# A four-stage language-model tower on one Trainium2 core: index-decoding blocks at other heads, feed-forward outputs added bank by bank, own PSUM banks at the entry of block attention, the next normalisation inside its last rounds, and the output stored by tile

## The chip, the cores and the metric

The kernel runs on one core of one Trainium2 chip. Five engines of the core work side by side and meet only at semaphores: TensorE (PE in the profile), VectorE (DVE), ScalarE (ACT), GpSimd (POOL), and SyncE (SP), which issues the DMAs. The metric is the device time of one execution in microseconds (us), the median of several runs.

## The reference, cut to what matters

```python
h = tok_ref(x, Wq, Wk)                       # 4 layers of causal attention over one-hot tokens
h = h + attn_ref(layernorm(h), ...)          # RWKV time mixing, 16 heads of 128, scan over time
h = h + ffn_ref(layernorm(h), w1, b1, w2, b2)    # ternary weights, gelu, 512 -> 2048 -> 512
h = h + moba_ref(layernorm(h), Wq, Wk, Wv, Wo)   # block attention, 16 heads of 128
h = h + glu_ref(layernorm(h), lut, gate_idx, up_idx, down_idx)  # silu(gate) * up, weights lut[idx]
```

There are 2048 tokens (8 sequences of 256) of width 512. In the last stage the three weight matrices (1376 x 512 each) are given as indices into a table of 16 numbers.

## The kernel before, in words

`h` (float32) stays in SBUF as 16 tiles of 128 tokens; four tiles are a chunk `c` of 512 tokens, so each stage runs over chunks 0 to 3. Nearly all products are made from a float16 high part and a float16 low part of each operand: one operand's tile is evicted from PSUM by ScalarE (high part) and then by VectorE (low part, value minus high part), and three matmuls (`PASSES`) take the place of one. PSUM has eight banks of 128 x 512 float32; which bank a tile uses decides what it must wait for. The order on every engine is written out by hand; an engine's queue is in order, so that whatever stands behind a waiting instruction waits too.

**Normalisation** (`ln_*`), per chunk: VectorE takes statistics of the four tiles (`bn_stats`, `bn_aggr`, `rstd`), GpSimd raises to -0.5, VectorE writes the normalised tile (`ln_dve_x`), TensorE transposes it (`ln_pe`, four float32 transposes, line 523), ScalarE and VectorE evict the two halves into `tokT` (`ln_act`, line 531; `ln_dve_lo`, line 538). `e` numbers the 64 tiles of the four normalisations.

**Decoding blocks.** The weights of the last stage are decoded by VectorE in blocks of 256 columns (`dec_block`, lines 802 to 820) that are put between other work: after the heads in `RW_DEC` (time mixing) and in `FF_DEC` (feed-forward). SyncE stores each block (`store_dec`) between its own loads of weights.

**Feed-forward**: 64 steps `t`, step `t` being head `t % 16` of chunk `t // 16`. TensorE does `ff_pe_proj(t)` (8 matmuls), then `ff_pe_out(t - 4)` (8 matmuls into banks 4 to 7, summed over the 16 heads of the chunk). After a chunk's last head VectorE adds the four banks to `h` (`ff_dve_acc`), and TensorE may begin the next chunk's first output into these banks only then. GpSimd makes the ternary weights just ahead (`ternary`).

**Block attention**: 64 rounds, two passes `p` of eight steps `s` of four heads `j`. One round on TensorE: queries of the next head (line 239, 12 matmuls), a tile of values for the next step (`mo_v`, 12), keys (12, with the transposes of the probabilities, line 261, after the first three), attention times values (line 1112), a tile of the previous step's output (`mo_out`, 12), the next scores. VectorE's softmax chain stands between the scores and the transposes. In the last step (`p` = 1, `s` = 7) there is no `mo_v`. At the entry the values of step 0 are made (four tiles, all in bank `VB`) and chunk 3 is normalised before the first round. After the last round come four output tiles (`mo_out_tail`).

**Gated stage** (`gl_*`): 12 units, each a group of weight tiles and a chunk. TensorE projects unit `t + 1`, then makes the outputs of unit `t`. Between them, before the change, the normalisation of one chunk each. VectorE decodes 18 more blocks meanwhile.

Of the kernel before, what the change touches and what calls it, by code (L numbers as in the profile page):

```python
# [14 lines left out]
P = 128  # L15
# [4 lines left out]
CH = 512  # L20
# [48 lines left out]
def build(nc, a):  # L69
    with ExitStack() as ctx:  # L70
# [42 lines left out]
        def encR(half_, tt):  # L113
# [83 lines left out]
        h_ps, g32, g_hi, g_lo, ff_out, ff_acc = (sem(x) for x in (  # L197
            "h_ps", "g32", "g_hi", "g_lo", "ff_out", "ff_acc"))
# [546 lines left out]
        def rw_dve_acc(dve, c):  # L745
            dve.wait_ge(rw_out, HEADS * (c + 1))
            for j in range(TPC):
# [4 lines left out]
                  (0, 1, 3, 4, 5, 6, 7, 12, 13, 14, 15), (0, 3, 6, 9, 12, 15)]  # L752
        FF_DEC = (3, 11, 17, 20, 25, 28, 33, 36, 41)
# [166 lines left out]
        def ff_pe_out(pe, t):  # L920
# [52 lines left out]
        def ff_pe(pe):  # L973
# [14 lines left out]
            for t in range(NF - FF_LAG + 1, NF):  # L988
# [77 lines left out]
        def mo_v(pe, p, s, j):  # L1066
# [27 lines left out]
        TAIL_BANK = [FB, 0, 1, 2]  # L1094
# [34 lines left out]
        def mo_pe(pe, p, s, j, nround, nstep, rcond, scond):  # L1129
            u = mo_u(p, s, j)  # L1130
            with Maybe(pe, rcond):
                mo_q(pe, *nround, 0)
            with Maybe(pe, scond):
                mo_v(pe, *nstep, j)
            if rcond is None:
                mo_q(pe, *nround, 1, lambda: pe_transpose_probs(pe, u))
            else:
                pe_transpose_probs(pe, u)
                with Maybe(pe, rcond):
                    mo_q(pe, *nround, 1)  # L1140
            if s == 0 and j == 0:
# [894 lines left out]
```

## Time and profile before

| | |
|---|---|
| median of 3 runs | 2507.6 us |
| lowest, highest | 2503.48, 2508.18 us |
| the profiled execution, its own time | 2510.17 us |
| span of the profiled execution | 2508.2 us |
| TensorE busy | 2341.0 us, 93% of the span |
| VectorE busy | 1651.7 us, 66% |
| ScalarE busy | 788.6 us, 31% |
| GpSimd busy | 371.9 us, 15% |

The span runs from the first to the last event of the profile. TensorE is busy nearly everywhere, so the rows to look at are those where it is not: a row of the timeline has, in brackets at its end, how long the engine was idle before it and what released it.

### The profile page before, as it was taken

To read this page: it belongs to the slowest core of one execution; us is meant where nothing else is said; L and a number is where in the kernel's file an instruction comes from. 1 tells how busy PE (TensorE), PEld (TensorE's weight loads), DVE (VectorE), ACT (ScalarE), POOL (GpSimd) and SP (SyncE) were. 2 spreads that over 40 slices of the span, in tenths; PEclk is the share of its full clock that TensorE was granted. 3 is DMA by queue.
4 is the path that set the end of the run, shared out by engine and by line. 5 is a ranking of instruction groups with operands and counts; after the bars stand their busy time and mean duration, and the time that the engine had idled before them with its cause. 6 is when DMAs were issued, how large, how long until landed. Compare 5 with 4: busy or idle time off the path is not lost.

```text
span 2508.2 us, 32499 instructions
## 1 busy us (share of the span) xinstructions
PE 2341.0 (93%) x12610; PEld 1208.1 (48%) x12610; DVE 1651.7 (66%) x3165; ACT 788.6 (31%) x1683; POOL 371.9 (15%) x416
## 2 busy tenths in 40 slices
PE   5877699999999998989989999999999997899999
PEld 3665344444444444434445555555555544444444
DVE  6665599998999777785345555555555565678622
ACT  5565513112122122333333333333333332211111
POOL 2362200000000411630040004002200300400000
PEclk9998899999999999999989999999999998999999
DMA  4545533333332441211010001000100100000001
GB/s 159 182 149 173 186 123 110 126 122 110 122 118 84 160 160 34 76 34 40 1 67 1 1 1 68 1 2 18 51 1 1 51 1 38 18 1 1 1 1 68
DMA packets 50751, 166.71 MB, mean 66 GB/s; under 512 B 4000, under 2 KB 16928, under 8 KB 41632
## 3 DMA queue, kind: packets, MB, share of 16 engines
q1 hardware_dynamic: 50592, 164.56, 18.6%
q8 instruction: 103, 1.69, 0.3%
q14 instruction: 56, 0.46, 0.1%
HBM read 137.28 MB, written 27.26 MB: 66 GB/s over the span
## 4 chain that ended last, share of the span: by engine, by line
PE 81%; DVE 11%; ACT 4%; issue 2%; POOL 1%; DMA 1%; SPq 0%; DVEq 0%; ACTq 0%
PE ps L665 19%; PE ps L239 13%; PE ps L1240 7%; PE ps L1078 7%; PE ps L677 6%; PE ps L1091 6%; PE ps L558 4%; PE ps L933 3%; PE ps L916 3%; PE ps L408 2%; PE ps L253 2%; PE ps L261 2%; PE ps L1112 2%; PE ps L251 1%; PE ps L523 1%
## 5 line engine op out<-in xcount | busy, mean ns | idle before, releaser
L665 PE MATMUL ps<-planes 128*128 128x512 f16 x1224 | 270.0, 379 | 1.5 <-DVE work L722 1.5
L665 PE MATMUL ps<-planes,wa 128*128 128x512 f16 x1080 | 237.8, 379 | 0.8 <-DVE wsc L1863 0.8
L239 PE MATMUL ps<-planes,wa 128*128 128x512 f16 x840 | 200.0, 383 | 5.1 <-DVE planes L1486 5.1
L665 PEld LDWEIGHTS ps<-planes 128*128 128x128 f16 x1224 | 119.6, 98 | 143.4 <-DVE work L722 2.4
L239 PE MATMUL ps<-planes 128*128 128x512 f16 x768 | 183.1, 382 | 1.3 <-issue 1.3
L705 ACT ACTIVATE work<-work 128x512 f16<-128x512 f32 x64 | 40.3, 630 | 439.8 <-DVE work L738 439.8
L665 PEld LDWEIGHTS ps<-planes,wa 128*128 128x128 f16 x1080 | 105.5, 98 | 125.8 <-DVE wsc L1863 0.8
L294 ACT ACTIVATE ps<-ps,nmax 128x128 f32<-128x128 f32 x160 | 54.4, 340 | 312.1 <-DVE nmax L288 312.1
L505 POOL TENSOR_TENSOR rstd<-rstd,half 128x4 f32<-128x4 f32 x16 | 17.2, 1072 | 889.7 <-DVE rstd L500 889.7
L802 DVE TENSOR_SCALAR work<-work,lutx,par 128x256 int32<-128x256 int32 x384 | 136.0, 429 | 0.0
L820 DVE COPY_PREDICATED work<-work 128x1024 f32<-128x1024 int16 x144 | 121.2, 842 | 22.0 <-DVE work L820 1.3
L933 PE MATMUL ps<-wa,work 128*128 128x512 f16 x512 | 123.8, 387 | 5.4 <-DVE h L958 5.4
L916 PE MATMUL ps<-planes,wa 128*128 128x512 f16 x512 | 124.0, 387 | 3.7 <-POOL wa L1038 3.7
L239 PEld LDWEIGHTS ps<-planes,wa 128*128 128x128 f16 x840 | 82.8, 99 | 92.3 <-DVE planes L1486 5.5
L1240 PE MATMUL ps<-planes 128*128 128x512 f16 x528 | 119.6, 386 | 2.8 <-DVE planes L538 2.8
L1240 PE MATMUL ps<-planes,wa 128*128 128x512 f16 x528 | 116.6, 379 | 0.0
L239 PEld LDWEIGHTS ps<-planes 128*128 128x128 f16 x768 | 75.7, 99 | 80.2 <-issue 4.3
L318 DVE TENSOR_TENSOR work<-ps,work 128x768 f16<-128x768 f32 x76 | 72.7, 956 | 58.4 <-ACT work L314 58.4
L677 PE MATMUL ps<-planes,work 128*128 128x512 f16 x408 | 95.1, 383 | 7.3 <-DVE work L743 7.3
L1078 PE MATMUL ps<-planes 128*128 128x512 f16 x384 | 91.1, 388 | 8.1 <-DVE planes L1178 5.5
L1184 DVE TENSOR_TENSOR h<-ps,h 128x512 f32<-128x512 f32 x64 | 44.2, 692 | 81.6 <-PE ps L1091 77.9
L886 POOL TENSOR_SCALAR planes<-stg 128x512 f16<-128x512 f32 x44 | 29.8, 705 | 436.4 <-PE ps L1091 431.2
(192 smaller groups left out, 4326.4 us busy)
## 6 DMA issues: line engine op xcount, KB each, us to landing
planes<-rw SPq DMA_DIRECT2D x17, 2048.0 KB, 7.8
wa<-rw SPq DMA_DIRECT2D x15, 2048.0 KB, 7.2
stg<-in_rw_w SPq DMA_DIRECT2D x32, 512.0 KB, 3.9
stg<-in_ff_w SPq DMA_DIRECT2D x16, 1024.0 KB, 5.1
rw<-wa SPq DMA_DIRECT2D x16, 1024.0 KB, 6.9
stg<-in_mo_w SPq DMA_DIRECT2D x16, 1024.0 KB, 4.8
work<-in_glu_idx SPq DMA_DIRECT2D x48, 128.0 KB, 2.1
glu_dec<-work SPq DMA_DIRECT2D x48, 128.0 KB, 1.7
```

The source lines that it names most:

```text
L239: mm = te.matmul(ps[:, bank, :], w(i, kt), x(j, kt), start=(kt == 0 and n == 0), stop=(kt == KT - 1 and n == 2))
L318: ve.tensor_tensor(pT[1].rearrange("p (b k) -> p b k", b=2), pT_view, pT[0].rearrange("p (b k) -> p b k", b=2), ALU.subtract).then_inc(pT_ ...
L558: mm = te.matmul(ps[:, bank, :], x, y, start=(m == 0), stop=(m == len(pairs) - 1))
L665: mm = te.matmul(ps[:, what, :], rw_w(q, what, i, kt, m), mix[what][j][:, kt, at:at + CH], start=(kt == 0 and z == 0), stop=(kt == KT - 1 ...
L677: mm = te.matmul(ps[:, 4 + j, :], oT[t % 4][x][:, j * P:j * P + P], rw_wo(q, y, m), start=(n == 0 and z == 0), stop=(n == HEADS - 1 and z ...
L802: return ve.tensor_scalar(dec_v[:, j, :].bitcast(I32), dec_idx, lutx[:, j:j + 1], lut[:, 2 * j:2 * j + 1], ALU.bitwise_and, ALU.bitwise_xor)
L820: ins = ve.copy_predicated(pairs[:, :, 0, :], mask, pairs[:, :, 1, :])
L916: mm = te.matmul(ps[:, t % 3, :], slot[:, at:at + P], tokT[x][:, kt, c * CH:c * CH + CH], start=(kt == 0 and x == 0), stop=(kt == KT - 1 a ...
L933: mm = te.matmul(ps[:, 4 + j, :], gT[t % FF_BUF][x][:, j * P:j * P + P], slot[:, PW + m * D:PW + m * D + D], start=(k == 0 and x == 0), st ...
L1078: mm = te.matmul(ps[:, VB, :], tokT[x][:, kt, tt * P:tt * P + P], halves(slot, 2)[y][:, kt * CH:kt * CH + CH], start=(kt == 0 and z == 0), ...
L1091: mm = te.matmul(ps[:, FB, :], x, y, start=(z == 0), stop=(z == len(pairs) - 1))
L1240: mm = te.matmul(ps[:, bank, :], glu_halves(g, piece)[i][:, at:at + P], tokT[j][:, kt, c * CH:c * CH + CH], start=(kt == 0 and z == 0), st ...
```

## The change

Six things are altered.

1. The decoding blocks of the last time-mixing chunk stand after heads 0, 3, 6, 8, 11, 13 (before: 0, 3, 6, 9, 12, 15), those of the feed-forward stage after steps 3, 15, 17, 21, 31, 34, 38, 47, 50 (before: 3, 11, 17, 20, 25, 28, 33, 36, 41).
2. In the feed-forward stage VectorE adds each bank as soon as that bank is complete, and TensorE waits bank by bank.
3. At the entry of block attention the four value tiles get banks 3 to 6, the first is made before the last two feed-forward outputs, and the transposes of chunk 3 get banks 7, 4, 5, 6.
4. The normalisation of chunks 0 and 1 for the gated stage is done in the last eight rounds (`s` = 6, 7), one tile a round, its statistics one tile a round from `s` = 5. This is inside `If` blocks that only the last pass enters. Chunk 2 is normalised among the tail outputs, chunk 3 among the projections of unit 1.
5. The tail outputs use banks 7, 6, 2, 3 (before: 7, 0, 1, 2).
6. The last chunk of the result is stored in four DMAs, one a tile.

```diff
-                  (0, 1, 3, 4, 5, 6, 7, 12, 13, 14, 15), (0, 3, 6, 9, 12, 15)]
-        FF_DEC = (3, 11, 17, 20, 25, 28, 33, 36, 41)
+                  (0, 1, 3, 4, 5, 6, 7, 12, 13, 14, 15), (0, 3, 6, 8, 11, 13)]
+        FF_DEC = (3, 15, 17, 21, 31, 34, 38, 47, 50)
...
         def ln_bank(e):
+            if e < 4:
+                return ps[:, 6 + e % 2, :]
+            if e < 44:
+                return ps[:, 3, :]
+            if e < 48:
+                return ps[:, (7, 4, 5, 6)[e - 44], :]
+            return ps[:, 4 if e < 56 else 4 + e % 2, :]
...
         def ff_pe_out(pe, t):
-            elif k == 0:
-                pe.wait_ge(ff_acc, TPC * c)
             pe.wait_ge(g_lo, t + 1)
             for j in range(TPC):
+                if c > 0 and k == 0:
+                    pe.wait_ge(ff_acc, TPC * (c - 1) + j + 1)
...
+                if k == HEADS - 1 and j < TPC - 1:
+                    mm.then_inc(ff_bank, 1)
             mm.then_inc(ff_out, 1)
...
         def ff_dve_acc(dve, c):
-            dve.wait_ge(ff_out, HEADS * (c + 1))
             dve.wait_ge(b2_added, TPC * (c + 1))
             for j in range(TPC):
+                if j < TPC - 1:
+                    dve.wait_ge(ff_bank, (TPC - 1) * c + j + 1)
+                else:
+                    dve.wait_ge(ff_out, HEADS * (c + 1))
...
         def mo_pe(pe, p, s, j, nround, nstep, rcond, scond):
+            def transposes():
+                if s > 6 or (s == 6 and j > 0):
+                    with last_pair(pe, p, MO_PAIRS):
+                        pe.wait_ge(ln_done, 24 + 4 * s + j)
+                pe_transpose_probs(pe, u)
...
+            if s == 0 and j == 0:
+                pe.wait_ge(ln_done, 48)
...
+            if s >= 6:
+                with last_pair(pe, p, MO_PAIRS):
+                    ln_pe(pe, 3, s - 6, j)
             with Maybe(pe, rcond):
                 pe_scores(pe, mo_u(*nround))
...
         def mo_dve(dve, p, s, j, nround, nstep, rcond, scond, chain):
+            if s >= 6:
+                with last_pair(dve, p, MO_PAIRS):
+                    ln_dve_x(dve, 3, s - 6, j)
...
                 mo_dve_acc(dve, p, s, j)
+            if s >= 6:
+                with last_pair(dve, p, MO_PAIRS):
+                    ln_dve_lo(dve, 3, s - 6, j)
             with Maybe(dve, rcond):
                 dve_max(dve, mo_u(*nround))
                 dve_norm(dve, mo_u(*nround))
+            if s >= 5:
+                with last_pair(dve, p, MO_PAIRS):
+                    dve.wait_ge(mw_acc, 8 + 49 + 4 * (s - 5) + j)
+                    chain(ve.bn_stats(stat[:, j, :], h[:, (s - 5) * TPC + j, :]))
+                    if j == TPC - 1:
+                        ln_dve_rstd(dve, 3, s - 5, chain)
...
-            for c in range(NC):
+            for c in range(NC - 1):
                 sp.wait_ge(wo_acc, 2 + O_GL + 4 * (2 * NC + c) + 4)
...
+            for tt in range(NT - TPC, NT):
+                sp.wait_ge(wo_acc, 2 + O_GL + 4 * 2 * NC + tt + 1)
+                sp.dma_start(a["out"][:, tt:tt + 1, :], h[:, tt:tt + 1, :]).then_inc(out_sem, 16)
```

How instructions move on VectorE at the end of time mixing: heads 13 to 15 of the last chunk, of before. Lines 722 to 738 are one head, line 538 the low half of a transposed tile, 743 the low part that TensorE's output product reads, 802 and 820 belong to a decoding block, 951 is the first low part of the feed-forward stage.

```order
L722 TENSOR_TENSOR work<-work,ps 128x2x256
L743 TENSOR_TENSOR work<-work 128x512
L729 SCALAR_TENSOR_TENSOR work<-wdec,work 128x256 x2
L734 SCALAR_TENSOR_TENSOR work<-work,par 128x512
L738 TENSOR_TENSOR work<-work 128x512
L538 TENSOR_TENSOR planes<-ps,planes 128x4x128
L807 CAST work<-work 128x256
...
L802 TENSOR_SCALAR work<-work,lutx,par 128x256 x8
...
L743 TENSOR_TENSOR work<-work 128x512
L951 TENSOR_TENSOR work<-work 128x512 x2
```

The same place after the change (the line numbers are those of the changed kernel: 752 is what 743 was, 747 was 738, 547 was 538, 962 was 951).

```order
L731 TENSOR_TENSOR work<-work,ps 128x2x256
L752 TENSOR_TENSOR work<-work 128x512
L738 SCALAR_TENSOR_TENSOR work<-wdec,work 128x256 x2
L743 SCALAR_TENSOR_TENSOR work<-work,par 128x512
L747 TENSOR_TENSOR work<-work 128x512
L547 TENSOR_TENSOR planes<-ps,planes 128x4x128
L752 TENSOR_TENSOR work<-work 128x512
L962 TENSOR_TENSOR work<-work 128x512 x2
```

The block no longer stands between head 15 and the last low part. Next, VectorE at the entry of block attention, of before: 958 adds the feed-forward outputs, 1178 is the low part of a value tile, 284 to 288 the row maximum, 495 to 514 the normalisation, 301 to 307 the division by the row sum.

```order
L958 TENSOR_TENSOR h<-ps,h 128x512 x4
L1178 TENSOR_TENSOR planes<-ps,planes 128x512
L284 TENSOR_TENSOR ps<-ps,causal 128x256
...
L288 TENSOR_REDUCE nmax<-ps 128x2
L495 BN_STATS stat<-h 128x6 x4
L498 BN_AGGR mv<-stat 128x2 x4
L500 TENSOR_SCALAR rstd<-mv 128x4
...
L307 TENSOR_TENSOR work<-ps,rinv 128x2x256
L1178 TENSOR_TENSOR planes<-ps,planes 128x512 x3
L514 TENSOR_SCALAR work<-h,mv,rstd 128x512 x4
L538 TENSOR_TENSOR planes<-ps,planes 128x4x128 x4
```

And of the changed kernel (1209 is what 1178 was, 972 was 958, 499 to 521 are the normalisation, 547 was 538).

```order
L1209 TENSOR_TENSOR planes<-ps,planes 128x512
L972 TENSOR_TENSOR h<-ps,h 128x512 x4
L499 BN_STATS stat<-h 128x6 x4
L505 BN_AGGR mv<-stat 128x2 x4
L507 TENSOR_SCALAR rstd<-mv 128x4
L1209 TENSOR_TENSOR planes<-ps,planes 128x512 x2
L521 TENSOR_SCALAR work<-h,mv,rstd 128x512 x4
L1209 TENSOR_TENSOR planes<-ps,planes 128x512
L284 TENSOR_TENSOR ps<-ps,causal 128x256
...
L288 TENSOR_REDUCE nmax<-ps 128x2
L547 TENSOR_TENSOR planes<-ps,planes 128x4x128 x4
```

The normalisation now stands ahead of the value tiles 1 to 3 and of the softmax. Last, TensorE after the last round, of before: 1104 are the tail outputs, 523 transposes, 1240 projections, 558 outputs.

```order
L1104 MATMUL ps<-wa,planes 128x512 x48
L523 MATMUL ps<-ident,work 128x128 x16
L1240 MATMUL ps<-planes 128x512 x96
L523 MATMUL ps<-ident,work 128x128 x16
L1240 MATMUL ps<-planes 128x512 x96
L523 MATMUL ps<-ident,work 128x128 x16
L558 MATMUL ps<-planes,work 128x512 x48
```

And of the changed kernel (532 is what 523 was, 1123 was 1104, 1285 was 1240).

```order
L532 MATMUL ps<-ident,work 128x128 x8
L1123 MATMUL ps<-wa,planes 128x512 x12
L532 MATMUL ps<-ident,work 128x128 x4
L1123 MATMUL ps<-wa,planes 128x512 x12
L532 MATMUL ps<-ident,work 128x128 x4
L1123 MATMUL ps<-wa,planes 128x512 x24
L1285 MATMUL ps<-planes 128x512 x120
L532 MATMUL ps<-ident,work 128x128 x4
L1285 MATMUL ps<-planes 128x512 x24
```

Eight transposes now stand ahead of the first tail output, and no transposes stand between the outputs and the projections.

## Rows read from the trace of the kernel before

**Rows 1.** The page's first line, the span and the instruction count.

```profile
span 2508.2 us, 32499 instructions
```

**Rows 2.** Busy time by stretch of the span, columns as in its first line.

```profile
core 0: us, PE busy (x) PEld busy (x) DVE busy (x) ACT busy (x) POOL busy (x), PEclk, DMA share, GB/s
965.00:1240.00 275.00, 252.71 (x1161) 116.32 (x1159) 184.43 (x335) 97.08 (x149) 73.57 (x84) 0.96 0.12 41
1240.00:1280.00 40.00, 23.33 (x88) 10.41 (x89) 17.69 (x32) 7.67 (x17) 26.80 (x32) 0.74 0.22 79
1280.00:2007.00 727.00, 724.14 (x4317) 394.99 (x4315) 404.77 (x721) 267.54 (x720) 77.45 (x91) 1.00 0.05 18
2007.00:2114.00 107.00, 91.43 (x534) 49.65 (x532) 58.28 (x113) 34.96 (x98) 2.02 (x2) 0.95 0.00 1
2114.00:2241.00 127.00, 109.86 (x498) 52.59 (x499) 88.79 (x197) 24.67 (x41) 31.11 (x38) 0.92 0.07 27
2241.00:2509.00 268.00, 259.52 (x1199) 116.77 (x1197) 137.40 (x283) 39.25 (x64) 13.07 (x24) 0.99 0.04 16
```

**Rows 3.** TensorE's timeline, feed-forward stage: start, length, line, operation, [idle before <-releaser].

```profile
983.21 4.22 PE L677 MATMUL ps<-planes,work 128*128 128x512 f16 x12 [7.29 <-DVE work L743]
...
1023.08 3.00 PE L916 MATMUL ps<-planes,wa 128*128 128x512 f16 x8 [3.71 <-POOL wa L1038]
...
1057.14 2.93 PE L933 MATMUL ps<-wa,work 128*128 128x512 f16 x8 [1.97 <-DVE h L958]
...
1095.12 0.83 PE L523 MATMUL ps<-ident,planes 128*128 128x128 f32 x4 [4.80 <-DVE planes L538]
...
1126.07 3.58 PE L933 MATMUL ps<-wa,work 128*128 128x512 f16 x8 [2.31 <-DVE h L958]
...
1186.05 1.90 PE L933 MATMUL ps<-wa,work 128*128 128x512 f16 x8 [1.11 <-DVE h L958]
```

**Rows 4.** VectorE's timeline, feed-forward stage, and one row of GpSimd's.

```profile
1046.84 0.29 DVE L807 CAST work<-work 128x256 int16<-128x256 int32 x1
...
1053.40 1.28 DVE L951 TENSOR_TENSOR work<-work 128x512 f16<-128x512 f32 x2
...
1061.66 6.44 DVE L802 TENSOR_SCALAR work<-work,lutx,par 128x256 int32<-128x256 int32 x8
...
1179.45 0.69 DVE L951 TENSOR_TENSOR work<-work 128x512 f16<-128x512 f32 x1 [2.76 <-ACT work L947]
...
1003.23 1.38 POOL L505 TENSOR_TENSOR rstd<-rstd,half 128x4 f32<-128x4 f32 x1 [25.01 <-DVE rstd L500]
```

**Rows 5.** TensorE's timeline at the entry of block attention.

```profile
1242.35 4.35 PE L1078 MATMUL ps<-planes 128*128 128x512 f16 x12 [2.58 <-DVE h L958]
...
1280.11 2.75 PE L1078 MATMUL ps<-planes 128*128 128x512 f16 x12
```

**Rows 6.** TensorE's timeline in the rounds, and one row of VectorE's.

```profile
1690.56 2.75 PE L239 MATMUL ps<-planes 128*128 128x512 f16 x12 [1.30 <-issue]
...
2078.90 0.87 PE L261 MATMUL ps<-ident,work 128*128 128x128 f32 x6 [1.69 <-DVE work L307]
...
2052.54 0.69 DVE L1178 TENSOR_TENSOR planes<-ps,planes 128x512 f16<-128x512 f32 x1 [0.37 <-ACT planes L1158]
...
2054.05 0.96 DVE L318 TENSOR_TENSOR work<-ps,work 128x768 f16<-128x768 f32 x1 [0.83 <-ACT work L314]
```

**Rows 7.** TensorE's and VectorE's timelines after the last round.

```profile
2114.47 10.52 PE L1104 MATMUL ps<-wa,planes 128*128 128x512 f16 x48 [0.88 <-DVE h L1184]
...
2186.55 1.94 PE L523 MATMUL ps<-ident,work 128*128 128x128 f32 x8 [5.78 <-DVE planes L538]
...
2240.60 20.88 PE L1240 MATMUL ps<-planes 128*128 128x512 f16 x96
...
2117.53 1.92 DVE L514 TENSOR_SCALAR work<-h,mv,rstd 128x512 f32<-128x512 f32 x4
```

**Rows 8.** VectorE's timeline, its last row.

```profile
2502.79 0.69 DVE L563 TENSOR_TENSOR h<-ps,h 128x512 f32<-128x512 f32 x1 [1.25 <-PE ps L558]
```

More of the change, by code:

```diff
@@ L496, in ln_dve_chunk, with ln_dve_rstd @@
             chain(ins)
+            ln_dve_rstd(dve, f, c, chain)
+        def ln_dve_rstd(dve, f, c, chain):
             for j in range(TPC):
@@ L987, in ff_pe @@
             mo_q(pe, 0, 0, 0, 1)
-            for t in range(NF - FF_LAG + 1, NF):
+            ff_pe_out(pe, NF - FF_LAG + 1)
+            pe.wait_ge(ln_done, 44)
+            mo_v(pe, 0, 0, 0, V_FIRST[0])
+            for t in range(NF - FF_LAG + 2, NF):
                 ff_pe_out(pe, t)
@@ L1064, in mo_q, with mo_v @@
                        lambda i, kt: tokT[i][:, kt, c * CH:c * CH + CH], between)
-        def mo_v(pe, p, s, j):
+        V_FIRST = [3, 4, 5, 6]
+        def mo_v(pe, p, s, j, bank=VB):
             g, c = s // 4, s % 4
@@ L1135, in mo_pe @@
             if rcond is None:
-                mo_q(pe, *nround, 1, lambda: pe_transpose_probs(pe, u))
+                mo_q(pe, *nround, 1, transposes)
             else:
-                pe_transpose_probs(pe, u)
+                transposes()
                 with Maybe(pe, rcond):
                     mo_q(pe, *nround, 1)
-            if s == 0 and j == 0:
-                pe.wait_ge(ln_done, 48)
             mo_pv(pe, p, s, j)
@@ L1876, in _ @@
             dve_k(dve, MU)
+            mo_dve_v(dve, 0, 0, 0, V_FIRST[0])
             ff_dve_acc(dve, NC - 1)
-            mo_dve_v(dve, 0, 0, 0)
-            dve_max(dve, MU)
             dve.wait_ge(ff_acc, TPC * NC)
             ln_dve_chunk(dve, 2, NC - 1, chain)
-            dve_norm(dve, MU)
-            for j in range(1, TPC):
-                mo_dve_v(dve, 0, 0, j)
-            ln_chunk(dve, ln_dve_x, 2, NC - 1)
-            ln_chunk(dve, ln_dve_lo, 2, NC - 1)
-            def mo_dve_round(p, s, j, *rest):
-                mo_dve(dve, p, s, j, *rest)
-                if s >= 5 and j == 3:
-                    with last_pair(dve, p, MO_PAIRS):
-                        dve.wait_ge(mw_acc, 8 + 52 + 4 * (s - 5))
-                        ln_dve_chunk(dve, 3, s - 5, chain)
-            mo_rounds(dve, mo_dve_round)
-            ln_chunk(dve, ln_dve_x, 3, 0)
-            for tt in range(TPC):
-                mo_dve_acc(dve, MO_PAIRS, 0, tt, TAIL_BANK[tt])
-            ln_chunk(dve, ln_dve_lo, 3, 0)
+            mo_dve_v(dve, 0, 0, 1, V_FIRST[1])
+            mo_dve_v(dve, 0, 0, 2, V_FIRST[2])
+            ln_chunk(dve, ln_dve_x, 2, NC - 1)
+            mo_dve_v(dve, 0, 0, 3, V_FIRST[3])
+            dve_max(dve, MU)
+            ln_chunk(dve, ln_dve_lo, 2, NC - 1)
+            dve_norm(dve, MU)
+            mo_rounds(dve, lambda *x: mo_dve(dve, *x, chain))
+            ln_chunk(dve, ln_dve_x, 3, 2)
+            ln_dve_lo(dve, 3, 2, 0), ln_dve_lo(dve, 3, 2, 1)
+            mo_dve_acc(dve, MO_PAIRS, 0, 0, TAIL_BANK[0])
+            ln_dve_lo(dve, 3, 2, 2)
+            mo_dve_acc(dve, MO_PAIRS, 0, 1, TAIL_BANK[1])
+            ln_dve_lo(dve, 3, 2, 3)
+            mo_dve_acc(dve, MO_PAIRS, 0, 2, TAIL_BANK[2])
+            mo_dve_acc(dve, MO_PAIRS, 0, 3, TAIL_BANK[3])
             dve.wait_ge(mw_acc, 8 + 64)
             ln_dve_chunk(dve, 3, 3, chain)
-            ln_chunk(dve, ln_dve_x, 3, 1)
+            ln_chunk(dve, ln_dve_x, 3, 3)
             def gdec_step(t, at):
```

86 lines of the change are left out of this document (47 added, 39 removed).

## The prediction

> **What bounds the kernel now.** I read busy time by stretch first: TensorE sets the pace, and what can be won is where it stands still or runs at the lower clock. Of the span of 2508.2 us [rows 1], the rounds of block attention up to 2007 leave it idle 3 us in 727; nothing is to be had there. The feed-forward stretch (965 to 1240) leaves 22 us, the entry of block attention (1240 to 1280) 17 in 40, at a granted clock of 0.74, the last rounds (2007 to 2114) 16 of 107, the stretch after them (to 2241) 17 of 127, and the rest 8 [rows 2]. Then TensorE's timeline, for each idle time and its releaser: nearly always VectorE, which is behind because a decoding block or a normalisation stands ahead of what TensorE needs. A full-speed group of 8 matmuls of 512 columns takes 1.73 us to the next start, one of 12 takes 2.59; these follow from the starts in the rounds, and behind a wait of 2 us or more the rows are longer (4.22, 3.00, 2.93 and 3.58 us where 2.75 and 1.89 are usual) [rows 3]: the lower clock costs some 1.7 us each time.
>
> **Step a, the end of time mixing.** A block ahead of the last low part holds TensorE 7.29 us, and the 12 matmuls behind it take 4.05 to the next start instead of 2.59 [rows 3]. With the last block after head 13, VectorE has 4.9 us of slack to absorb it, and the low part is done in time: 7.3 + 1.5 = 8.8. Is it given back at the next wait, step 12's weights from GpSimd (3.71 us, [rows 3])? GpSimd stood 25.01 us waiting for the statistics that VectorE takes behind step 4 [rows 4]. These come earlier with the rest, so the wait moves along and stays near 4. I take 8.6. Were GpSimd bound by its weights alone, 0 to 3 would be left.
>
> **Step b, blocks in the feed-forward stage, and bank-by-bank sums.** A block with GpSimd at rest takes 6.56 us (1046.84 to 1053.40); beside GpSimd's splits its eight leaf instructions alone take 6.44 [rows 4], as long as the whole. TensorE can wait for a sum at three places, the first output of chunks 1 to 3. Bank by bank, the first bank is free 0.62 us after VectorE starts instead of 2.48: 1.9 better wherever VectorE is late. But where VectorE is late is set by the blocks. Chunk 1: blocks at 15 and 17 lie so close that the second starts some 1.5 us late and meets GpSimd's split; the sum starts 1056.5 to 1057.5 against 1054.6, the first bank is free at 1058.2, against 1057.14 [rows 3]: 1.0 lost. Chunk 2: the block at 34 is followed by one low part and the sum: TensorE would wait 2.95 instead of 2.31: 0.65 lost. Chunk 3 had no block near; TensorE waited 1.11 [rows 3]. Now low part 50 starts at 1179.45 [rows 4], +0.6 the block, to 1186.6, low part 51, first bank at 1187.85, while TensorE is ready at 1184.94: 2.9 instead of 1.1, plus the lower clock 1.6: 3.4 lost. Against these, the wait of 4.80 at the second transpose of chunk 0 with its slow row [rows 3] goes, as no block stands at 25; the first transpose waits some 3 us longer for block 21: 2.2 won. Sum of b: -2.9, bounds -9 (the first-transpose wait long, each chunk slow) and +4 (blocks hidden by the banks).
>
> **Step c, entry of block attention.** Before: TensorE ends the feed-forward outputs at 1239.8, then four value tiles, each waiting for the eviction of the last (one bank), and four transposes likewise (2.58 idle before the first tile, [rows 5]); the first value tile of round 1 starts at 1280.11 [rows 5]. After, worked forward from 1239.8: value tile 0 stands ahead of the last 16 matmuls, so outputs end at 1242.4; scores to 1243.4; tiles 1 to 3 without a wait (the first bank is added by 1241.7, the last by 1243.6) to 1251.2. VectorE: statistics to 1246.7, GpSimd's power 1.1, two low parts, normalised tiles from 1249.9 at 1.1 to 1.3 each, as GpSimd is splitting. Transposes at 1251.2, 1252.1, 1253.2, and the last at 1255.0 behind low part 3. Softmax maximum to 1256.8, four low halves to 1259.5. TensorE does round 1's queries from 1255.6, slow, to 1260.1, and then the value tile. 1280.1 - 1260.1 = 20. Bounds 14 and 22.
>
> **Step d, the last rounds.** TensorE gets eight groups of four float32 transposes; six such in a row take 0.87 us with their tail, 0.71 to the next start [rows 6], so a group takes 0.47 when fast, the last more: 3.9 in all. In the four rounds of step 7 the softmax is exposed: TensorE waits 1.69 us for it [rows 6]. The low half (0.6 us, as 0.69 with its tail in [rows 4]) now stands ahead of the maximum; it ends about 0.25 us after the scores do: 1.0 for four. In step 6 the added 1.1 us (statistics 0.6, normalised tile 0.5) fall in front of the low part of the probabilities, before which VectorE was idle 0.83, and 0.37 two instructions ahead of it [rows 6]: 1.2 of cover, less the 0.25; I count 0.3 for three rounds. The three former groups of statistics (a wait of 1.6 to 1.7 us each, within the 16 us of this stretch, [rows 2]) become a group with GpSimd's power in the middle: the same. d = -5.2, bounds -4 and -12.
>
> **Step e, from the last round to unit 3.** Counted from the end of the last round's output, 2113.6. Before: the projection of unit 3 starts at 2240.6 [rows 7], 127.0 later. After: work of four tail tiles 10.4, three projections 62.2, two outputs 20.7, eight groups of transposes 3.5 = 96.8. New waits: the first transpose needs one low half, statistics, power and a normalised tile, about 5.0 us after the last output, against 0.9 before the tail [rows 7]; 4.3 idle after one group of transposes. Lower clock 2.5 (two slow groups), small waits 1, an allowance. Together 105. So e = 22. The idle 5.78 us [rows 7] and its like one unit later vanish: they were VectorE, which now has 4 normalised tiles of 0.48 us [rows 7] and 4 low halves of 0.6 [rows 4] fewer there. I take 21.5, bounds 15 and 23.
>
> **Step f, the store.** The last sum ends at 2503.5 [rows 8], the span 4.7 later: issue and a transfer of 1 MB. A 256 KB transfer should land in 2.2 to 2.8 after issue: 1.7, bounds 0.5 and 2.5.
>
> **Branches.** The `If` blocks add some 15 compare-and-branch a pass on TensorE, 28 on VectorE. The rounds before hold such branches too, and are idle 3 us in 727 [rows 2]. Only the jump back of the loop shows, 1.30 us [rows 6]. I take 1 for all. The Trainium skill (Advanced Engine Details and Errata, Control Flow Timing) gives about 108 ns for a compare-and-branch and 51 ns for a plain one; if nothing hid them, TensorE's 30 would cost some 5 us by that page, an estimate, and the sum be 4 us smaller. The trace of the rounds speaks for hidden.
>
> **Sum.** 8.6 - 2.9 + 20 - 5.2 + 21.5 + 1.7 - 1 = 42.7. The profiled execution took 2510.2 by its own time, which gives 2467.5; the median of the runs shown is 2.6 lower, 2507.6, and lies within their spread, so 2465.
>
> **The rivals.** *The likeliest*: gains of 30 to 50 us, 2457 to 2478: 0.76.
> *VectorE becomes late where it has just been loaded.* In rounds of step 7 TensorE would idle 1.94 us, close to the 1.97 after which its rows were slow [rows 3, 6]: 1.7 more each for three rounds; with b at its bound and c at 14: gain 42.7 - 5 - 6 - 6 - 3 = 23, some 2485. For it: VectorE's cover in step 6 is 0.1 us wide. Against: most idle times that are removed are waits by construction. 0.13 (2478 to 2500).
> *The change frees more than I count*: no slow rows at the entry, blocks hidden: 2450 to 2457: 0.07.
> *Slower: the added branches are not hidden.* If each of TensorE's 30 cost what the jump back costs, 1.30 us [rows 6], that is 39 us; with VectorE's in the softmax chain it is above 43 and the kernel comes out at 2508 to 2520. It decides from 1.45 us a branch. Against it: the branches already in the rounds. 0.02. A smaller cost of that kind leaves no change, 0.01; below all that, 0.01.
> *A part doesn't do what it says*: the bank-by-bank sums are covered by the blocks ahead of them, worth nothing at chunks 2 and 3; this is in b.
>
> **How the numbers follow.** Prediction 2465, range 2452 to 2484: the likeliest case, the better one in part, and half of the late one. A difference of 0.2%, 5 us, is about what a measurement here can tell from none. Faster 0.96, within 0.02, slower 0.02.
>
> **What the profile after would show.** a: no idle time in front of line 677's successor at 975. b: waits for `h` at three chunk starts, the third near 2.9 us. c: value tiles back to back, round 1's value tile 20 us nearer to the last feed-forward output. d: rounds of step 6 near 13.6 us, those of step 7 near 13.2. e: one idle time of 4 us ahead of the tail, then none above 1 until unit 3; 105 us from the last round's output to unit 3. f: 3 us from the last sum to the end. It is wrong if GpSimd's weights at step 12 come no earlier, if step-7 rounds run slow, or if the tail waits for more than the statistics.

## The result, and the profile after

| | before | after |
|---|---|---|
| median (4 runs each, in one comparison) | 2507.89 us | 2475.82 us |
| lowest, highest | 2503.48, 2510.07 | 2473.06, 2478.94 |
| ratio, 95% interval | | 0.9873, 0.9857 to 0.9889 |
| profiled execution, own time / span | 2510.17 / 2508.2 | 2473.06 / 2471.1 |

The change gains 32.1 us by the medians, 37.1 by the two profiled spans; forecast were 42.7, a time of 2465 in a range of 2452 to 2484. The profiled execution of after was the fastest of its kernel, that of before slower than all four of its row: 3.2 of the 37.1 us are there before the change has moved anything on TensorE (the time-mixing output at 966.68 before stands at 963.45 after).

Busy time by stretch first (with [rows 2], columns as there): the feed-forward stage, and the entry of block attention, which now lies between 1233 and 1252.

```profile
965.00:1233.00 268.00, 250.50 (x1149) 115.16 (x1148) 169.82 (x318) 97.90 (x150) 75.57 (x84) 0.96 0.12 41
1233.00:1252.00 19.00, 15.87 (x87) 8.14 (x84) 16.04 (x29) 6.91 (x16) 12.16 (x15) 1.00 0.12 44
```

At the entry the granted clock was 0.74 with 17 us idle in 40; now it is 1.00 with 3 idle in 19. The feed-forward stretch still has 17.5 idle. What TensorE waits for, from the view of waits (us in total, times, longest):

```profile
PE ps L942 <- DVE h L972: 9.0, 3, 3.1
PE ps L567 <- DVE h L572: 8.1, 6, 5.3
PE ps L532 <- DVE planes L521: 6.6, 5, 4.5
...
PE ps L925 <- POOL wa L1055: 4.0, 1, 4.0
PE ps L1285 <- DVE work L1323: 2.6, 2, 2.1
```

Lines 567 and 1285 are the gated stage's outputs and projections, and the forecast had no wait of 5.30 or 2.13 us there. TensorE's timeline in the feed-forward stage (with [rows 3]):

```profile
975.11 5.34 PE L925 MATMUL ps<-planes,wa 128*128 128x512 f16 x24
...
1011.21 3.27 PE L925 MATMUL ps<-planes,wa 128*128 128x512 f16 x8 [3.98 <-POOL wa L1055]
...
1045.79 2.31 PE L942 MATMUL ps<-wa,work 128*128 128x512 f16 x8 [2.82 <-DVE h L972]
...
1066.41 1.12 PE L532 MATMUL ps<-ident,planes 128*128 128x128 f32 x4 [4.49 <-DVE planes L521]
...
1113.95 3.57 PE L942 MATMUL ps<-wa,work 128*128 128x512 f16 x8 [3.11 <-DVE h L972]
...
1177.09 3.04 PE L942 MATMUL ps<-wa,work 128*128 128x512 f16 x8 [3.10 <-DVE h L972]
...
1222.06 5.34 PE L239 MATMUL ps<-planes 128*128 128x512 f16 x24
```

The 7.29 us of [rows 3] are gone (step a), and every chunk's first output waits for its sum longer than before (step b). The rows behind two of these waits are slow: 3.57 us at a granted clock of 0.50 and 3.04 at 0.63. The one of chunk 1, 2.31 us, is not: its granted clock is 1.00. It has to wait for VectorE bank by bank, three more banks at 0.62 us each and 0.45 for its last two matmuls, and it takes the same 2.31 us in experiments 1 and 5 behind waits of 0.49, 0.61 and 1.29. The entry (with [rows 5]):

```profile
1235.99 7.93 PE L1097 MATMUL ps<-planes 128*128 128x512 f16 x36
...
1244.74 0.63 PE L532 MATMUL ps<-ident,work 128*128 128x128 f32 x4 [0.37 <-DVE work L521]
...
1247.84 0.66 PE L532 MATMUL ps<-ident,work 128*128 128x128 f32 x4 [1.18 <-DVE planes L1209]
...
1252.16 2.75 PE L1097 MATMUL ps<-planes 128*128 128x512 f16 x12 [1.07 <-DVE planes L547]
```

Three value tiles stand in one row, no wait reaches 1.2 us and no row is slow. The last rounds, step 7 (with [rows 6]):

```profile
2054.40 0.94 PE L261 MATMUL ps<-ident,work 128*128 128x128 f32 x6 [1.93 <-DVE work L307]
2055.14 3.77 PE L239 MATMUL ps<-planes,wa 128*128 128x512 f16 x9
```

The wait for the softmax is 1.93 where it was 1.69, and behind one of three such waits nine matmuls took 3.77 us for 2.10, at a granted clock of 0.55. From the last round on, TensorE, then VectorE and GpSimd beside it (with [rows 7]):

```profile
2095.93 1.92 PE L532 MATMUL ps<-ident,work 128*128 128x128 f32 x8 [4.30 <-DVE work L521]
...
2109.77 26.06 PE L1285 MATMUL ps<-planes 128*128 128x512 f16 x120
...
2144.01 5.35 PE L1285 MATMUL ps<-planes 128*128 128x512 f16 x24 [2.13 <-DVE work L1323]
...
2155.87 5.34 PE L567 MATMUL ps<-planes,work 128*128 128x512 f16 x24
2166.51 7.62 PE L567 MATMUL ps<-planes,work 128*128 128x512 f16 x24 [5.30 <-DVE h L572]
...
2205.79 20.88 PE L1285 MATMUL ps<-planes 128*128 128x512 f16 x96
```

```profile
2091.23 0.69 DVE L1215 TENSOR_TENSOR h<-ps,h 128x512 f32<-128x512 f32 x1 [1.98 <-PE ps L1110]
...
2133.54 1.14 DVE L857 TENSOR_SCALAR planes<-planes 128x256 int16<-128x256 int16 x1
...
2143.28 0.68 DVE L1323 TENSOR_TENSOR work<-work,ps 128x512 f32<-128x512 f32 x1
...
2146.18 0.23 DVE L857 TENSOR_SCALAR planes<-planes 128x256 int16<-128x256 int16 x1
...
2165.77 0.68 DVE L572 TENSOR_TENSOR h<-ps,h 128x512 f32<-128x512 f32 x1
...
2467.96 0.69 DVE L572 TENSOR_TENSOR h<-ps,h 128x512 f32<-128x512 f32 x1 [1.25 <-PE ps L567]
```

```profile
2133.45 4.55 POOL L899 TENSOR_TENSOR wa<-stg,wa 128x512 f16<-128x512 f32 x4
```

TensorE makes two output tiles of unit 0 from 2155.87 and then waits 5.30 us, since the third goes into the bank of the first, which VectorE adds only at 2165.77. VectorE had no idle time above 0.7 us since 2132.8 and is behind. The first decoding block of this stage is one reason: it fills 2132.81 to 2143.28, 10.5 us, where in the kernel before it took 6.2 (2159.40 to 2165.62). Its small instructions take 1.14 to 1.26 us where the first of these lines takes 0.23 at 2146.18, and four of them fill 4.58 us beside four instructions of GpSimd that fill 4.55. The Trainium skill (SBUF — State Buffer, SBUF: two separate sides) says that VectorE and GpSimd share a pair of ports under a lock that one of them holds for a whole instruction, where VectorE's instruction is in a two-port mode or has two inputs in SBUF. The 4.58 against 4.55 us for four each agree with it; of which kind these four are, no run here shows. In the kernel before, GpSimd's splits ended at 2156.5, ahead of that block:

```profile
2151.46 5.00 POOL L890 TENSOR_TENSOR wa<-stg,wa 128x512 f16<-128x512 f32 x4
```

The 37.1 us by the prediction's steps, each from its marker in the one trace to that in the other:

| step | forecast | measured | markers, before and after |
|---|---|---|---|
| before any change | 0 | 3.2 | 966.68, 963.45 |
| a, end of time mixing | 8.6 | 8.9 | 24 matmuls of line 916 / 925: 987.26, 975.11, less 3.2 |
| b, feed-forward | -2.9 | -5.0 | from there to the first queries: 241.98, 246.95 |
| c, entry | 20 | 20.8 | queries to round 1's value tile: 50.87, 30.10 |
| d, last rounds, branches | -6.2 | -5.6 | to VectorE's sum of the last round: 833.52, 839.07 |
| e, to unit 3 | 21.5 | 12.4 | 126.97, 114.56 |
| f, to the end | 1.7 | 2.3 | 267.6, 265.3 |

### The profile page after: what moved, and what is told of

It reads as the page before. It is cut to its first block, busy times and chain, and to the rows that moved or that the text cites. A ratio compares the mean times of both kernels' runs of the same rounds, so it can differ in the third digit from the quotient of the medians.

```text
span 2471.1 us, 32609 instructions
## 1 busy us (share of the span) xinstructions
PE 2327.8 (94%) x12610; PEld 1203.5 (49%) x12610; DVE 1652.3 (67%) x3165; ACT 788.4 (32%) x1683; POOL 374.4 (15%) x416
## 3 DMA queue, kind: packets, MB, share of 16 engines
q8 instruction: 103, 1.69, 0.3%
## 4 chain that ended last, share of the span: by engine, by line
PE 80%; DVE 11%; ACT 5%; issue 2%; POOL 1%; DMA 1%; SPq 0%; DVEq 0%; ACTq 0%
PE ps L674 19%; PE ps L239 13%; PE ps L1285 7%; PE ps L686 7%; PE ps L1110 6%; PE ps L1097 6%; PE ps L567 3%; PE ps L925 3%; PE ps L942 3%; PE ps L408 2%; PE ps L253 2%; PE ps L1131 2%; PE ps L261 2%; PE ps L251 1%; PE ps L532 1%
## 5 line engine op out<-in xcount | busy, mean ns | idle before, releaser
L674 PE MATMUL ps<-planes 128*128 128x512 f16 x1224 | 270.0, 379 | 1.2 <-DVE work L731 1.2
L239 PE MATMUL ps<-planes 128*128 128x512 f16 x768 | 180.9, 379 | 1.5 <-issue 1.5
L1285 PE MATMUL ps<-planes 128*128 128x512 f16 x528 | 116.9, 379 | 2.6 <-DVE work L1323 2.6
L962 DVE TENSOR_TENSOR work<-work 128x512 f16<-128x512 f32 x64 | 49.4, 783 | 73.9 <-ACT work L958 73.9
L301 DVE RECIPROCAL rinv<-rsum 128x4 f32<-128x4 f32 x80 | 14.2, 177 | 119.4 <-ACT ps L296 119.4
```

The costliest lines, as they stand in the source:

```text
L239: mm = te.matmul(ps[:, bank, :], w(i, kt), x(j, kt), start=(kt == 0 and n == 0), stop=(kt == KT - 1 and n == 2))
L674: mm = te.matmul(ps[:, what, :], rw_w(q, what, i, kt, m), mix[what][j][:, kt, at:at + CH], start=(kt == 0 and z == 0), stop=(kt == KT - 1 ...
L1285: mm = te.matmul(ps[:, bank, :], glu_halves(g, piece)[i][:, at:at + P], tokT[j][:, kt, c * CH:c * CH + CH], start=(kt == 0 and z == 0), st ...
```

## The experiments

The changed kernel is at 0.9873 of before; 0.001 is 2.5 us. Ratios are to the kernel before, run on the same chip, and gains against the changed kernel are differences of two such ratios. As each is known to about 0.0016, a difference is good to some 5 us. Experiments 1, 2, 5 and 10 to 12 are clear of the changed kernel; the intervals of 3, 4, 6 and 8 touch or overlap its own, so there the same stretch in two traces is given as well.

**1. The old feed-forward table.**

```diff
-        FF_DEC = (3, 15, 17, 21, 31, 34, 38, 47, 50)
+        FF_DEC = (3, 11, 17, 20, 25, 28, 33, 36, 41)
```

> The changed kernel (2475.8 us) with the feed-forward blocks back after steps 3, 11, 17, 20, 25, 28, 33, 36, 41; the bank-by-bank sums stay. Theory (the new table made the feed-forward stage slower, the sums by bank made it faster): the waits for h at the starts of chunks 1 to 3, now 2.82, 3.11 and 3.10 us, shrink below 0.5 each as 1.9 comes off the 1.97, 2.31 and 1.11 of the kernel before, their slow rows go, and the wait of 4.8 at the second transpose of chunk 0 comes back in place of 4.49 at the first: about 11 us less, 2465. Rival (the sums by bank bring nothing, the tables alone tell): the three waits are 2.0, 2.3 and 1.1 as in the kernel before, 5 us less, 2471.

2465.49 us, 0.9823 (0.9807 to 0.9840): 12.5 us faster than the changed kernel. TensorE's timeline:

```profile
1047.31 2.31 PE L942 MATMUL ps<-wa,work 128*128 128x512 f16 x8 [0.49 <-DVE h L972]
...
1067.26 1.12 PE L532 MATMUL ps<-ident,planes 128*128 128x128 f32 x4 [3.83 <-DVE planes L521]
...
1114.55 2.31 PE L942 MATMUL ps<-wa,work 128*128 128x512 f16 x8 [0.61 <-DVE h L972]
```

With the old table the sums by bank cut 1.97 and 2.31 to 0.49 and 0.61, and 1.11 to nothing. The 4.80 at the second transposes of chunk 0 did not come back as I expected: the first ones wait 3.83, the second 2.15. The stretch of step b takes 236.15 us, against 241.98 before and 246.95 after: edit 2 alone is worth 5.8 us, the new table costs 10.8.

**2. Sums of whole chunks.** Edit 2 is undone, the new tables stay.

```diff
-                if c > 0 and k == 0:
-                    pe.wait_ge(ff_acc, TPC * (c - 1) + j + 1)
+            elif k == 0:
+                pe.wait_ge(ff_acc, TPC * c)
```

> The changed kernel (2475.8 us) with its new tables, but TensorE waits for all four banks at the start of a chunk and VectorE for the whole chunk. Theory (1.9 us per chunk start): the three waits for h grow from 2.8, 3.1 and 3.1 to some 4.7, 5.0 and 5.0: 6 us more, 2482. Rival (what the prediction named: covered by the block ahead of the sum, worth nothing): 2476.

2487.10 us, 0.9909 (0.9891 to 0.9926): 9 us slower. The waits for `h` are 4.54, 4.80 and 4.80, and the one for the first normalised tile is 8.47 instead of 4.49:

```profile
1077.59 1.12 PE L532 MATMUL ps<-ident,planes 128*128 128x128 f32 x4 [8.47 <-DVE planes L521]
...
1126.73 3.59 PE L942 MATMUL ps<-wa,work 128*128 128x512 f16 x8 [4.80 <-DVE h L967]
```

So it is 1.7 us more for each chunk start, and the wait for the first normalised tile grew by 4.0 with them. The stretch of step b takes 257.01 us against 246.95: behind the new table the sums by bank are worth 10.1 us. That they are worth nothing behind a block is refuted.

**3. Four banks for the gated stage's outputs.**

```diff
-                out_tile(pe, O_GL + 4 * t + j, 6 + j % 2, pairs)
+                out_tile(pe, O_GL + 4 * t + j, GL_BANK[j], pairs)     # GL_BANK = [6, 7, 4, 5]
```

> The changed kernel (2475.8 us) with the gated stage's outputs in banks 6, 7, 4, 5 instead of 6 and 7 in turn, so that the third output tile of a unit does not wait until VectorE has added the first. Theory (a wait for a buffer, VectorE has slack after it): the waits for h in the gated stage, 8.1 us in all with 5.30 at unit 0, and the slow row behind it (7.62 for 5.34) go, and some 3 come back as waits for products: 7 us less, 2469. Rival (VectorE is the bound of units 0 and 1, the wait only moves to the products): 2475.

2468.48 us, 0.9843 (0.9826 to 0.9861): 7.5 us faster by the ratios, and from VectorE's last sum of the rounds to unit 3 it takes 107.09 us instead of 114.56. The four tiles are one row, and nothing comes back at unit 2's products. The product wait of unit 1 stays, and this time the row behind it is slow (6.99 for 5.34):

```profile
2146.05 6.99 PE L1290 MATMUL ps<-planes 128*128 128x512 f16 x24 [2.12 <-DVE work L1328]
...
2158.93 10.52 PE L572 MATMUL ps<-planes,work 128*128 128x512 f16 x48
```

**4. No decoding block in unit 0**, three each in units 1 to 6.

```diff
-                b = 3 * t - 2 + (at // 2 if at < 4 else 2) if t > 0 else 0
+                b = 3 * t - 3 + (at // 2 if at < 4 else 2) if t > 0 else GDEC_BLOCKS
```

> The changed kernel (2475.8 us) without a decoding block in unit 0 of the gated stage: the 18 blocks stand three each in units 1 to 6. Theory (the first block, 10.5 us beside GpSimd's splits where 6.2 is usual, is what made VectorE late): the waits of TensorE for products, 2.13 and 0.44, go and the 5.30 at the third output tile of unit 0 is 1 to 2 shorter: 4 us less, 2472. Rival (the three blocks and four low halves of unit 1 are what makes it late): the product waits go, the output wait grows by as much, 2475.5.

2466.90 us, 0.9838 (0.9816 to 0.9860): 8.8 us faster by the ratios, twice what I expected; to unit 3 it takes 105.45 us instead of 114.56. The product waits are gone, and the 5.30 has become 1.41, with no slow row behind it:

```profile
2155.84 5.34 PE L567 MATMUL ps<-planes,work 128*128 128x512 f16 x24
2162.59 5.35 PE L567 MATMUL ps<-planes,work 128*128 128x512 f16 x24 [1.41 <-DVE h L572]
```

That block was thus the cause of most of VectorE's delay; I had taken too little off the output wait. The run takes away all of its 10.5 us, and does not part the 6.2 of the block from the 4.3 that it is longer beside GpSimd's splits.

**5. A new feed-forward table**: no block in the two steps before a chunk's sum, none between a sum and its normalised tiles.

```diff
-        FF_DEC = (3, 15, 17, 21, 31, 34, 38, 47, 50)
+        FF_DEC = (3, 12, 15, 27, 31, 41, 44, 57, 60)
```

> The changed kernel (0.9873 of before) with the feed-forward blocks after steps 3, 12, 15, 27, 31, 41, 44, 57, 60: none within two steps ahead of a chunk's sum, none between the sum and the normalised tiles. Theory (where VectorE is late is set by the place of the blocks): the waits for h, 2.82, 3.11 and 3.10, and the 4.49 for the normalised tiles go to below 1 each and their slow rows with them: 15 us less, 0.9815 of before, below the 0.9823 that the old table gave. Rival (GpSimd's splits, from 1040 to 1079 us, slow VectorE's own tiles, block or not): the 4.49 stays, 0.983.

2457.20 us, 0.9785 (0.9772 to 0.9799): 22 us faster by the ratios, more than expected. The stretch of step b takes 228.30 us, 18.7 less, and has three waits left, the 3.98 for GpSimd and these:

```profile
1045.53 2.31 PE L942 MATMUL ps<-wa,work 128*128 128x512 f16 x8 [1.29 <-DVE h L972]
...
1084.56 0.63 PE L532 MATMUL ps<-ident,planes 128*128 128x128 f32 x4 [0.87 <-DVE planes L547]
```

**6. Two tail outputs first**, in banks 3 and 2, ahead of the first transposes of chunk 2.

```diff
-            ln_pe(pe, 3, 2, 0), ln_pe(pe, 3, 2, 1)
             mo_out_tail(pe, 0, weight_slot("moba", 1))
+            mo_out_tail(pe, 1, weight_slot("moba", 1))
+            ln_pe(pe, 3, 2, 0), ln_pe(pe, 3, 2, 1)
...
```

> The changed kernel (0.9873 of before) with two tail outputs, in banks 3 and 2, ahead of the first transposes of chunk 2. Theory (the 4.30 us before these transposes is VectorE's statistics, power and normalised tiles, and 5.2 us of outputs cover it): the wait and the slow rows behind it (1.92 for the transposes, 3.65 for 2.75) go, 6 us less, 0.985. Rival (VectorE gets what TensorE no longer waits for as a debt to unit 1): the waits at unit 1's products and at the third output tile of unit 0 grow by about 3, half is given back, 0.986.

2471.93 us, 0.9850 (0.9833 to 0.9868): 5.8 us faster by the ratios. The 4.30 us are covered, the rows behind are fast, and the waits of unit 1 stay as they were (2.06, 5.30). From the start of the last round's output to unit 0 it takes 15.8 us, 22.1 in the changed kernel.

```profile
2094.59 5.34 PE L1124 MATMUL ps<-wa,planes 128*128 128x512 f16 x24
2099.77 1.04 PE L532 MATMUL ps<-ident,work 128*128 128x128 f32 x8
```

**7. One bank for value tiles 1 to 3 of the entry.**

```diff
-        V_FIRST = [3, 4, 5, 6]
+        V_FIRST = [3, 7, 7, 7]
...
-                pe.wait_ge(ff_acc, TPC * (NC - 1) + j)
+                pe.wait_ge(ff_acc, TPC * NC)
+                pe.wait_ge(mv_lo, j)
```

> The changed kernel (0.9873 of before) with value tiles 1 to 3 of the entry in one bank, each waiting for the eviction of the one ahead, and all for the last feed-forward sum; the order of the work stays. Theory (the banks and the order ahead each bring a part of the 20.8 us at the entry): each of three tiles waits 1 to 2.5 us, VectorE's normalised tiles stand ahead of the last, and the clock falls: 8 us more, 0.9905. Rival (VectorE's chain of statistics, tiles and low halves sets the end whatever the banks): within 2 us, 0.988.

2479.11 us, 0.9871 (0.9854 to 0.9888): no difference, my theory falls. The tiles do wait, but from the queries to round 1's value tile it is 31.99 us against 30.10:

```profile
1247.65 2.75 PE L1097 MATMUL ps<-planes 128*128 128x512 f16 x12 [1.50 <-DVE planes L1209]
...
1256.51 1.97 PE L532 MATMUL ps<-ident,work 128*128 128x128 f32 x16 [1.86 <-DVE planes L1209]
```

The waits of the value tiles run while VectorE makes the statistics and tiles that the transposes need anyway. Of the 20.8 us of step c the value tiles' own banks bring 1.9. The rest is left to the normalisation ahead of the softmax, the first value tile before the last outputs, and the transposes in banks of their own; which of these brings what is not shown.

**8. The last rounds as before**: edits 4 and 5 undone, all else kept (`mo_rounds` without the `If` blocks, chunks 0 and 1 normalised after the last round).

> The changed kernel (0.9873 of before) with edits 4 and 5 undone: the normalisation of chunks 0 and 1 again after the last round, no added branches, tail banks 7, 0, 1, 2. Theory (rows: 12.2 us gained from the last round to unit 3, 5.4 lost in the rounds): 7 us more, 0.990. Rival (edits 4 and 5 as predicted, 21.5 gained, with the losses elsewhere): 15 us more, 0.993.

2484.78 us, 0.9900 (0.9885 to 0.9915): 6.8 us slower, as 12.4 - 5.6 would have it. Its own trace has the way to unit 3 at 126.04 us (11.5 longer) and the rounds at 832.42 (6.7 shorter), 4.8 us in all. So edits 4 and 5 together gain 5 to 7 us and not the 15 of the forecast. The idle times at the second transposes are there again:

```profile
2159.32 1.77 PE L532 MATMUL ps<-ident,work 128*128 128x128 f32 x8 [4.94 <-DVE planes L547]
```

**9. The branches alone**, in the kernel before; the same on ScalarE, and at the other places on TensorE and VectorE.

```diff
+            if s >= 6:
+                with last_pair(pe, p, MO_PAIRS):
+                    pe.wait_ge(scale_done, 1)
```

> The kernel before (ratio 1) with nothing added but the If blocks of edit 4 at the same places in the rounds (TensorE 15 a pass, VectorE 28, ScalarE 8), holding only a wait for a semaphore that has long been reached. Theory (branches are hidden by the queue of instructions ahead of them): within 2 us of before, 0.9995 to 1.001. Rival (TensorE and VectorE stand still at each, as at the jump back of the loop, 1.30 us): 20 to 40 us more, 1.008 to 1.016; a rival with 0.108 us each, the figure of the Trainium skill, page Advanced Engine Details and Errata, Control Flow Timing: some 5 us, 1.002.

2510.83 us against 2510.03, 1.0007 (0.9996 to 1.0017). The added branches cost between nothing and 4 us by the times, and the rival with the jump back's price is out. The 5 us of the third case, 1.002, lie just above the interval. But 0.108 us for each of TensorE's 30, the figure that this case takes from the Trainium skill (Advanced Engine Details and Errata, Control Flow Timing), would make 3.2 us, an estimate, or 1.0013, which the times do not exclude. The traces speak against it: from round 1's value tile to VectorE's sum of the last round, with all the added branches inside, it takes 833.76 us against 833.52.

**10. Four mends together**: those of experiments 3, 4, 5 and 6.

> The changed kernel (0.9873 of before) with four edits together: the new feed-forward table, four output banks in the gated stage, no block in unit 0, two tail outputs first. Theory (each takes away waits of its own; banks and block share the wait of 5.30 us with its slow row, so they count once): 0.0088 + 0.0023 + 0.0048 less, 0.971. Rival (VectorE was the bound and each next wait comes out elsewhere): 0.975.

2435.44 us, 0.9702 (0.9688 to 0.9715), where 0.971 was expected. From unit 0 on TensorE's timeline has no idle time up to unit 3. The way there is 17.6 us shorter, where experiments 3, 4 and 6 alone took off 7.5, 9.1 and 6.6: 3 and 4 share a wait, as expected.

**11. And another order on GpSimd.** The power waits for VectorE's statistics; the next piece of weights needs nothing of it.

```diff
             ffn_piece(2, 0)
-            ln_pool_chunk(pool, 1, 3)
-            ffn_piece(2, 1), ffn_piece(3, 0), ffn_piece(3, 1)
+            ffn_piece(2, 1)
+            ln_pool_chunk(pool, 1, 3)
+            ffn_piece(3, 0), ffn_piece(3, 1)
```

> As the four mends together, and GpSimd makes the sixth piece of the feed-forward weights ahead of the power of chunk 3 (it stood 15.0 us waiting for that chunk's statistics with the piece already loaded). Theory (the 3.98 us before step 12 is a wait for GpSimd's order): the wait and the slow row behind it (3.3 for 1.9) go, 5 us less than the four mends, 0.969. Rival (the next load of weights, behind a stored block in SyncE's queue, sets it): the wait stays, 0.971.

2429.44 us, 0.9683 (0.9670 to 0.9696). The times alone hardly part this from the version before it, but in the trace the wait before step 12 (3.99 us there) is gone. GpSimd makes the piece while it used to stand, and still reaches the power in time:

```profile
984.74 2.42 POOL L1060 TENSOR_SCALAR wa<-stg 128x512 f16<-128x512 f32 x4
995.82 1.38 POOL L512 TENSOR_TENSOR rstd<-rstd,half 128x4 f32<-128x4 f32 x1 [8.67 <-DVE rstd L507]
```

**12. And the low half behind the maximum**, where VectorE waits for the exponentials.

```diff
+            with Maybe(dve, rcond):
+                dve_max(dve, mo_u(*nround))
             if s >= 6:
                 with last_pair(dve, p, MO_PAIRS):
                     ln_dve_lo(dve, 3, s - 6, j)
             with Maybe(dve, rcond):
-                dve_max(dve, mo_u(*nround))
                 dve_norm(dve, mo_u(*nround))
```

> The fastest version so far (0.9683 of before) with the low half of the transposed tile, in the rounds of steps 6 and 7, between the row maximum and the division instead of ahead of the maximum, where VectorE waits 1.78 us for ScalarE's exponentials. Theory (the low half ahead of the maximum costs 0.24 us a round, which makes 1.93 of a wait of 1.69, and now and then tips TensorE into slow rows): the waits for line 307 in step 7 go back to 1.69 and 4.93, the last nine rounds take 1.0 us less, 2.7 if the row of nine matmuls that took 3.77 us goes as well: 0.9675 to 0.968. Rival (something else sets the chain): waits stay 1.93, 0.9683.

2428.01 us, 0.9676 (0.9659 to 0.9693), the lowest median. The times can't tell it from the one before, the trace can: the softmax waits are 1.70 three times and 4.94, the nine matmuls behind all three take 2.11, and from the transposes of the first round of step 6 to the first ones after the last round it takes 102.1 us instead of 105.5. Of these 3.3 us some 1.4 are a slow row that experiment 11 has and this one has not; it comes and goes between the traces of one order of work (last section).

```profile
2034.20 0.87 PE L261 MATMUL ps<-ident,work 128*128 128x128 f32 x6 [1.70 <-DVE work L307]
2034.91 2.11 PE L239 MATMUL ps<-planes,wa 128*128 128x512 f16 x9
```

## Why the prediction was right in its direction and 9 us off in one step

**Steps a, c, f** came out as worked: 8.9 for 8.6, 20.8 for 20, 2.3 for 1.7 (the last sum ends 2.45 us before the span does, 3 were forecast). GpSimd's wait ahead of step 12 moved along with VectorE's statistics (3.98), and experiment 11 shows why: it is the order on GpSimd.

**Step b** had the three waits for a sum right (3.0, 2.95 and 2.9 by its sum, 2.82, 3.11 and 3.10 measured), but only one of its terms. Each place is counted here as its wait plus what the rows behind it take above the usual:

| place | won or lost, forecast | measured | before, after |
|---|---|---|---|
| chunk 1 | -1.0 | +0.4 | 3.7, 3.2 |
| transposes of chunk 0 | +2.2 | +0.1 | 7.4, 7.3 |
| chunk 2 | -0.65 | -2.0 | 4.0, 6.0 |
| chunk 3 | -3.4 | -3.8 | 1.1, 4.9 |

The transposes are the 2.1 us between -2.9 and -5.0: the wait for the normalised tiles, 4.49, is as long as the one it replaces (4.80), and three slow rows follow it. The four places make -5.2 before rounding, and the rest of the stretch gives 0.2 back. Chunks 1 and 2 miss by 1.4 each way, and that they cancel is luck: behind 2.82 us no row was slow, behind 3.11 two were. Experiment 1 settles the parts: sums by bank +5.8, table -10.8.

**Step d** was right in sum, in part by luck. Rounds of step 6 take 13.87 us (13.6 forecast): the transposes 0.44 and a wait of 0.27 for the low part of the probabilities, where I had counted 0.1. In step 7 a round takes 13.28 where nothing else happens (13.2 forecast). One slow row came as the rival of the late VectorE had it; its round is 14.68 us long, 1.4 more than the same round without one in experiment 1. Against these stands the 1 us for branches, of which experiment 9 shows 0.2. Experiment 12 shows the 0.24 us a round of the low half.

**Step e** failed, at the sentence "The idle 5.78 us [rows 7] and its like one unit later vanish: they were VectorE, which now has 4 normalised tiles of 0.48 us [rows 7] and 4 low halves of 0.6 [rows 4] fewer there". They were VectorE, but its decoding blocks, not its normalisation. In the kernel before, this is VectorE from the normalised tiles over the first block to the low halves that end the wait:

```profile
2157.58 1.91 DVE L514 TENSOR_SCALAR work<-h,mv,rstd 128x512 f32<-128x512 f32 x4
2159.40 0.29 DVE L846 CAST planes<-planes 128x256 int16<-128x256 int32 x1
...
2165.62 0.68 DVE L1274 TENSOR_TENSOR work<-work,ps 128x512 f32<-128x512 f32 x1
...
2185.72 1.28 DVE L538 TENSOR_TENSOR planes<-ps,planes 128x512 f16<-128x512 f32 x2
```

It goes from the start of unit 1's projection (2157.7) to the end of its third block (2185.7) without a pause but those for ScalarE's copies: 28.0 us for three blocks and four products, and of what the change takes away only 1.9 us of normalised tiles lie in it. After, the same way takes 35.3 us (2130.5 to 2165.8): VectorE is 2.3 us late to begin with, on unit 0's last product, the first block is 4.3 us longer beside GpSimd's splits, and the four low halves of chunk 3, 0.6 each, now stand between the blocks. TensorE was ready 30.7 us after the start, two waits for products included. So the wait only moved, from the second transposes to the third output tile, 5.30 for 5.78, and 2.13 and 0.44 at the products came to it. With the slow row (7.62 for 5.34) and 0.57 one unit later this is 10.7 us, where I had allowed 1 for small waits. The rest of the step came as worked: the wait ahead of the tail was forecast at 4.3 and is 4.30. Experiments 3 and 4 take most of the 10.7 away from either side, by banks and by the block (2.12 and 1.41 us of waiting are left), and 10 takes all of it.

## What to carry to other kernels

When an idle time of the leading engine is put down to a lagging one, list what fills the lagging engine up to that moment: if it is not what the change takes away, the wait only moves to the next place where the two meet. Where work of one engine is free to be placed, keep it away from the last steps ahead of a hand-over and from stretches in which an engine beside which it ran slower is busy; here the place of nine blocks was worth 18.7 us of a 247 us stretch, and all the mends together, which leave the work as it is and change only its order and its banks, 2.0%. Own buffers brought little where the same lagging engine holds the waiting one up right behind the wait anyway: three banks at the entry brought 1.9 us, two more at the gated outputs 7.5.

## What the runs showed of the hardware that was not expected

A wait of 1.93 us for the softmax was followed by nine matmuls of 2.10, 3.77 and 2.11 us in three rounds of one execution. Ten of the traces here have these three waits of 1.93 us. In six of them (the changed kernel, experiments 3, 4, 6, 10 and 11) the second of the three has a slow row behind it, 3.5 to 3.8 us, and in four (1, 2, 5 and 7) none has, though these rounds are the same in all. In the four traces in which the waits are 1.70 us (before, 8, 9 and 12) none of the twelve has one. That the shorter wait is the reason is likely and not shown.

Behind a wait of 2.82 us the granted clock stayed at 1.00; behind 3.11 and 3.10 it was 0.50 and 0.63 in the first row, which was 1.7 and 1.2 us longer than the usual 1.89. How slow the row behind a wait is varies with more than the length of the wait; what sets it stays open.

In the token stage, which no edit touches, the same row came out slow in one execution and fast in the other: 24 matmuls of line 408 behind a wait of 2.19 us took 4.45 us before, at a granted clock of 0.62, and 2.78 after, at 1.00. It is slow in twelve of the fourteen traces and fast in the changed kernel's and experiment 5's. Up to the first row of time mixing (299.33 before, 296.40 after) this and its like make 2.9 us. A sum of terms of a few us is to be compared stretch by stretch and not by two spans.
